# The bias product of the last graph layer on 128 rows in place of two

## What is computed

```python
h = relu(adj @ (ln(x) @ W1) + b1)
h = relu(adj @ (h @ W3) + b3)
x = x + tanh(h @ Wf + bf)                 # the bias bf is what the change touches
t = ln(x)
w, idx = top_k(t @ gate_w, 2);  w = softmax(w)
x = x + sum_e comb[:, e] * ((silu(t @ EW1[e]) * (t @ EW3[e])) @ EW2[e])
```

## Time and profile before

| | |
|---|---|
| median of 3 runs | 618.58 us (618.46 to 619.16) |
| the profiled execution | 617.84 us |
| its span | 616.0 us |
| PE busy | 577.4 us, 94% |
| PEld busy | 491.1 us, 80% |
| DVE busy | 373.5 us, 61% |
| ACT busy | 296.3 us, 48% |
| bias product, line 1522 | 16 times, 377 to 383 ns each |

### The profile page before, as it was taken

One profiled execution on the slowest core, in us unless ns is written; L12 is line 12 of the kernel. 1 busy time (PEld: TensorE's weight loads), 2 busy tenths in 40 slices (PEclk: granted clock), 3 DMA queues, 4 the chain that ended last, 5 costly groups with the idle time before them and its releaser, 6 DMA issues.

```text
span 616.0 us, 11115 instructions
## 1 busy us (share of the span) xinstructions
PE 577.4 (94%) x3248; PEld 491.1 (80%) x3249; DVE 373.5 (61%) x804; ACT 296.3 (48%) x561; POOL 144.8 (24%) x143
## 2 busy tenths in 40 slices
PE   2878999999999999999989999999999999999993
PEld 2766777787877877779878988988989889898873
DVE  5888878884666797567743333346333735566671
ACT  2654554565656484567423323354233635465461
POOL 3000000000000506036654233232222231222222
PEclk9999999999999999999999999999999999999998
DMA  9999990000212764431047222126211623646722
GB/s 200 225 224 215 215 215 17 0 1 0 104 35 68 145 179 166 137 104 19 2 77 256 37 36 33 22 34 221 34 26 26 189 68 79 183 97 167 221 34 28
DMA packets 66419, 63.73 MB, mean 103 GB/s; under 512 B 5914, under 2 KB 60828, under 8 KB 66364
## 3 DMA queue, kind: packets, MB, share of 16 engines
q1 hardware_dynamic: 57724, 52.32, 34.7%
q0 software_dynamic: 8224, 10.53, 10.5%
q10 hardware_dynamic: 432, 0.39, 0.2%
HBM read 54.02 MB, written 10.26 MB: 104 GB/s over the span
## 4 chain that ended last, share of the span: by engine, by line
PE 76%; DVE 9%; issue 5%; ACT 5%; DMA 3%; POOL 1%; SPq 1%; POOLq 0%; ACTq 0%; DVEq 0%
PE bank L1625 27%; PE bank L1651 14%; PE bank L1496 8%; PE bank L1498 7%; PE bank L1497 7%; PE bank L1679 4%; PE bank L1525 2%; DVE ring L978 2%; PE bank L1509 2%; DVE adj_s L1016 2%; DMA adj_s<-in_adj 1%; PE bank L1618 1%; ACT ring L648 1%; PE bank L1522 1%; ACT hTf L660 1%
## 5 line engine op out<-in xcount | busy, mean ns | idle before, releaser
L1625 PE MATMUL bank<-ew,xeT 128*128 128x512 f32 x840 | 202.2, 395 | 1.9 <-DVE ew L1333 1.4
L1625 PEld LDWEIGHTS bank<-ew,xeT 128*128 128x128 f32 x840 | 154.6, 188 | 33.4 <-issue 2.3
L1496 PE MATMUL bank<-ring,Z 128*128 128x512 f32 x256 | 104.4, 408 | 13.5 <-DVE ring L978 13.2
L1651 PE MATMUL bank<-ew,heT 128*128 128x256 f32 x840 | 109.1, 286 | 3.5 <-issue 2.4
L978 DVE TENSOR_TENSOR ring<-adj_s,ring 128x512 fp32r<-128x512 f32 x128 | 86.1, 682 | 39.4 <-ACT ring L648 38.2
L1651 PEld LDWEIGHTS bank<-ew,heT 128*128 128x128 f32 x840 | 102.9, 191 | 5.2 <-issue 3.7
L1498 PE MATMUL bank<-ring,Z 128*128 128x512 f32 x256 | 100.1, 391 | 0.0
L1497 PE MATMUL bank<-ring,Z 128*128 128x512 f32 x256 | 100.1, 391 | 0.0
L648 ACT CAST ring<-adj_s 128x512 fp32r<-128x512 f32 x128 | 76.8, 624 | 39.5 <-PE bank L1498 27.8
L522 POOL DMA_INDIRECT slot_rows<-val,route x32 | 36.2, 1130 | 206.7 <-issue 202.7
L555 POOL DMA_INDIRECT out<-y_st,idx_st x29 | 45.4, 1564 | 160.2 <-ACT y_st L806 153.4
(11 more groups left out here) (189 smaller groups left out, 557.8 us busy)
## 6 DMA issues: line engine op xcount, KB each, us to landing
w_raw<-in_L_ffn_W SPq DMA_DIRECT2D x24, 1024.0 KB, 5.7
adj_s<-in_adj SPq DMA_DIRECT2D x64, 256.0 KB, 6.3
x_in<-in_x SPq DMA_DIRECT2D x16, 128.0 KB, 5.7
x_res<-in_x SPq DMA_DIRECT2D x4, 512.0 KB, 3.6
out<-x SPq DMA_DIRECT2D x4, 512.0 KB, 4.3
ffn_in_rows<-x_res SPq DMA_DIRECT2D x4, 512.0 KB, 4.2
xg<-ffn_in_rows,idx POOLq DMA_INDIRECT x39, 3.0
Wg<-in_L_gnn_W SPq DMA_DIRECT2D x2, 256.0 KB, 3.3
```

Of the source, the lines that this page charges most:

```text
L1496: nc.tensor.matmul(a, zh, hi, start=(jb == 0), stop=False)
L1625: last = nc.tensor.matmul(out_ap, stat[:, sl, k, :], w_at(k, wl), start=(k == k0 and sl == wl == 0), stop=(k == k1 - 1 and sl == 1))
L1651: last = nc.tensor.matmul(y_p[:, 0:D], heT[:, sl, k, :], ew[:, o + 2 * H * wl + D * k:][:, 0:D], start=(k == sl == wl == 0), stop=(k == KH ...
```

## The change

`one_rows` and `bf_parts` grow from two rows to 128. All 128 rows of `one_rows` are ones. `bf_parts` is set to zero in all rows first, in two halves of 128 columns, and then rows 0 and 1 get the two parts of the bias as before. The product at line 1522 keeps its text and its 256 columns, and now runs over 128 rows.

```diff
-        bf_parts = sb("bf_parts", [2, D], F32R)
-        one_rows = sb("one_rows", [2, P], F32R)
+        bf_parts = sb("bf_parts", [P, D], F32R)
+        one_rows = sb("one_rows", [P, P], F32R)
...
                 sign = bf_sign[:, :]
-                nc.vector.tensor_scalar(one_rows[:, :], iota[0:2, :], 0.0, 1.0, ALU.mult, ALU.add)
+                nc.vector.tensor_scalar(one_rows[:, :], iota[:, :], 0.0, 1.0, ALU.mult, ALU.add)
+                for half in range(KD):
+                    nc.vector.tensor_scalar(bf_parts[:, half * P:(half + 1) * P], iota[:, :], 0.0, None, ALU.mult)
...
-                nc.vector.scalar_tensor_tensor(out=bf_parts[:, :], in0=bf_in[:, :], scalar=pcol[0:2, :],
+                nc.vector.scalar_tensor_tensor(out=bf_parts[0:2, :], in0=bf_in[:, :], scalar=pcol[0:2, :],
```

## The result

| | before | after |
|---|---|---|
| median | 618.52 us (618.01 to 619.16, 4 runs) | 614.79 us (614.44 to 615.36, 4 runs) |
| ratio, 95% interval | | 0.994 [0.9923, 0.9957] |
| span of the profiled execution | 616.0 us | 612.9 us |
| PE busy | 577.4 us | 574.4 us |

The change makes the kernel 3.7 us faster. The forecast was 5.5 us. The changed kernel was run twice more beside the kernel before, on other chips: 0.993 [0.991, 0.9951] and 0.9933 [0.9913, 0.9953]. So it is about 4 us, and 1.4 to 1.8 us of the forecast are missing.

A forecast was written before the change was run, and what follows sets the result against it. TensorE was taken as the bound (76% of the last-ending chain, busy 94%). -4.5 (pairs), -1.3 (block 3) and +0.25 (fills) gave -5.55 us: 612.3 us for the profiled execution, 613.0 for the median; range 612.2 to 614.8.

The forecast's parts named there:

- the gap and its cause: Around the 2-row bias product on TensorE: weight loads do not run ahead across a change from 128 rows to 2, or back.
- A pair: Two bias tiles between adjacency products, six pairs in blocks 0 to 2: 2.66 to 1.91 us, 0.75 saved each, 4.5 in all.
- block 3: Last column block of the second adjacency product, four bias tiles back to back on TensorE: 4.77 to 3.46 us, 1.3 saved.
- Rival 1: At the bias product: the gap has another cause and stays with 128 rows; 618.8 us, no measurable change; chance 0.06.
- rival 4: At the bias products: only the load is freed, a 0.09 us drain stays before each; 614.4 us; chance 0.15 with Rivals 3.
- Rival 2: At `split_bf` on VectorE: dear fills delay the ring product by 1.0 us, loads stay exposed; slower, 619.7 us; chance 0.04.
- the fills: Two added 128x128 VectorE operations at `split_bf`, 50.4 us, that TensorE waits for: +0.25 us for both (0.2 to 0.72).
- (a): First expert's second weight matrix, landing 218.0 us, ScalarE's use 219.51: slack of 1.5 us falls to about 0, nothing lost.
- (b): First slots' indices, issued 227.26 us, converted by VectorE at 232.79: 2.5 us of slack become 1.
- (c): GpSimd's last scatters and slot list: 3.91 us idle; its work shifts 4.5 against 5.8, leaving 2.6 us of slack.
- Rivals 3: At (a) or (b) a transfer becomes the limit, block 1's 1.5 us is lost; 614.5 us; chance 0.15 with rival 4.

The follow-up runs named there:

- experiment 9: Changed kernel with the bias product on the first 32, 64 or 96 rows, one run each: 618.44, 619.26 and 614.07 us beside 619.32 for the kernel before.
- 14: Changed kernel with SyncE issuing block 3's two stores only after the sixth gather of the first slots has landed: 613.24 us, ratio 0.9925 to the kernel before.
- 15: Changed kernel with block 3's two stores issued behind the gathers and both fills of bf_parts on GpSimd: 611.93 us, ratio 0.9908 to the kernel before.
- experiment 11: Changed kernel with GpSimd's first row addition moved behind the last eight scatters: 616.05 us, ratio 0.9964 to the kernel before.
- 10: Changed kernel without further edit, run again beside the kernel before: 614.26 us, ratio 0.993.
- 16: Changed kernel without further edit, run on one chip with the two kernels whose stores were moved: 614.19 us, ratio 0.9933 to the kernel before.
- the second group above: Executions with 96 or 128 rows in block 3 and unmoved stores; slot list's product starts 50.0 to 50.8 us behind block 3's first bias product.
- 12: Changed kernel with block 3's four bias products back on two rows: 613.95 us, ratio 0.9937 to the kernel before.
- 5: Changed kernel with GpSimd's first row addition behind the last eight scatters, on another chip: 617.6 us beside 623.26 for the kernel before, ratio 0.9916.
- 7: Changed kernel with block 3's bias products back on two rows, on another chip: 619.3 us beside 623.26 for the kernel before, ratio 0.993.
- 8: Changed kernel with fills on GpSimd and its first addition behind the scatters, on another chip: 619.36 us beside 623.26 for the kernel before, ratio 0.9919.

## Why the prediction was wrong

**Right: the gap and its cause.** The bias product's load didn't run ahead because of its row count. A pair went from 2.66 to 1.90 us (1.91 forecast). The stretches between the blocks' first bias products shrank by 1.52, 1.53 and 1.42 us, 4.47 in sum (4.5 forecast), block 3 by 1.32 (1.3 forecast). Rival 1 fell, and rival 4 too: a drain of 0.09 would show as 2.08 a pair. One step of the reasoning was too wide: the load does run ahead between 96 and 128 rows (experiment 9), so not every change of the row count stops it. Rival 2 put the fills at 0.36 each and the wider one at 0.26. All three together are 0.28.

**Right: the fills,** 0.28 us against 0.25.

**Right: places (a) and (b).** ScalarE starts on the second weight matrix at 218.86, 2.2 us behind its landing, and VectorE converts the indices at 231.93, 3.7 us behind theirs, neither with a wait of its own in the trace. The transfers landed sooner behind their issue or later from execution to execution (12.0 us for the matrix here, 14.3 in the earlier trace rows), so these slacks are samples too. Block 1's stretch keeps its full 1.53 us.

**Wrong: place (c).** The step that failed is: "Its own work before that starts from a VectorE step ahead of block 3's bias products, so it shifts by 4.5 against 5.8; 2.6 us of slack remain." The first half came true, 0.83 us behind the first bias product in every kernel. The second half took the 3.91 us of idle for a property of the kernel, and the length of GpSimd's work for fixed. The idle is one execution's: the repeat of the kernel before has 1.46 us.

```profile
295.27 1.01 POOL L522 DMA_INDIRECT slot_rows<-val,route  x1 [1.46 <-DVE val L1167]
```

And GpSimd's work from the first gather to the last scatters' start, without idle, grew to 32.6 us. It was 28.9 in the first execution before, which makes 2.0 more in the gathers and 1.7 in the scatters and the addition between; it was 31.3 in the repeat, which makes 0.8 and 0.5. So most of the 2.6 us of slack was never there in the repeat: 1.46 less block 3's 1.3 leaves 0.1. The gathers' part is shown by 14 and 15: block 3's faster products brought the store of `x` onto the second gather. With VectorE's last values ready at 32.08 us behind the first bias product (experiment 11) and GpSimd there at 33.44, the last scatters begin 1.36 us late, and the issue of the list comes 1.4 to 1.6 us later than in 14 and 15. This is block 3's whole saving. The scatters' part wasn't taken apart; the trace shows single scatters of 2.73 and 2.07 us there, where the first execution before has one of 2.10.

**The sum by what was measured:** -4.47 - 1.32 + 0.28 + 1.3 = -4.2 us, beside 3.7, 4.15 and 3.9 in the three comparisons. Rivals 3 and 4 named the right time, 614.5 and 614.4, for wrong reasons: the one had block 1's share lost at (a) or (b), the other a drain that isn't there. That 614.79 lies just inside the range, which reached up to 614.8 for their sake, is luck.

**Still open:** the fall of the clock near 54 us. It was seen in four of the twelve executions with a wait of 2.08 to 2.10 us there (the changed kernel, 10, 14 and 16) and in none of the seven with 1.81 to 1.83. From the ring product behind `split_bf` to the first bias product these four take 118.7 to 119.2 us, and 117.6 to 117.8 is the time of all sixteen others. So where it falls, 1.0 to 1.5 us are lost. That the fills bring it on is not shown: four of twelve against none of seven can be chance, and near 16 us the clock fell in five of the twenty executions, in four of them ahead of every changed instruction. It also fell behind the wait for the list in two of the six executions of the second group above, 16 (1.72 us of wait) and 96 rows (1.86), and not behind 1.29 to 1.45 in three and 2.08 in one; from there the twelve products of 16 take 4.58 us in place of 2.99 in 10:

```profile
308.96 4.58 PE L1627 MATMUL bank<-ew,xeT 128*128 128x512 f32 x12
```

How many of the timed runs have such falls isn't known, and they blur the comparison of 10 with 12 and of 14 with 15: the fills' part and the slot list's part of the missing time are told apart by the stretches, not by the medians. Nor was the stall of ScalarE in 5, 7 and 8 settled.

## What to carry to other kernels

Before a small product goes between full ones, look whether its weight load starts beside the product ahead of it; if it starts with its own, at 64 rows or fewer, zero rows up to 128 (96 did as well, in one execution) won 0.38 us a product here. A saving on the engine that sets the pace also moves the transfers that wait for it, while others, started from ahead of the saving, stay where they are: write down for each transfer that shifts which one it will then meet. Slack read from one execution is a sample; a saving that leans on it needs a second trace, or a look at the work in front of the idle.

## What the runs showed of the hardware

- A product of 256 columns on 2, 32 or 64 rows between 128-row ones costs 0.38 us more than one on 96 or 128; 0.32 and 0.31 us stand before and behind it in place of 0.23 and 0.12.
- The granted clock fell to 0.50 for 3 to 3.5 us behind a wait of 2.09 to 2.10 us in four executions, and stayed at 1.00 behind one of 2.08 to 2.10 us in eight, four of them (5, 7, 11, 12) of kernels equal to the changed one up to there. The length of the wait alone doesn't decide it.
- From the second indirect gather of 128 rows to the third it took 3.5 to 3.75 us, and 4.6 to 4.9 when a store of 512 KB was issued up to 0.5 us behind the second. With no such store near, the step from the first to the second took 3.6 to 4.3. The Trainium skill, "DMA: Bandwidth & Descriptors", section Queues, rings and completion order, says that a DMA engine with work from several queues serves them in turn, packet by packet. That fits, but no run here separates it from a limit of the memory.
